# Cross-attention probabilities split before they are transposed, and transposed by a DMA instead of by TensorE

## The chip, the cores and the metric

The kernel runs on one core of one Trainium2 chip. Times are device microseconds of a whole execution. Beside the runs that are timed there is one execution with the hardware profiler; its trace has a span, from the first to the last instruction.

## What is computed

One decoder layer on x of 8 x 112 x 256 and a context of 8 x 375 x 256, in float32, with a layer norm after each of three parts: self-attention over the batch axis of the projected heads with rotary positions (16 heads of 16), cross-attention to the context (16 heads of 64), and a mixture of 8 experts, two per token, plus a shared expert. The change lies in the cross-attention:

```python
xn = _layernorm(x, ln_gamma, ln_beta)
q = (xn @ w_q).reshape(B, SQ, NUM_HEADS, DIM_HEAD)
k, v = jnp.split(context @ w_kv, 2, axis=-1)
scores = jnp.einsum('bqhd,bkhd->bhqk', q * SCALE, k)
attn = jax.nn.softmax(scores, axis=-1)
out = jnp.einsum('bhqk,bkhd->bqhd', attn, v).reshape(B, SQ, INNER)
```

## The kernel before

Three blocks run one after the other: preparation (weights split into high and low parts), attention, and the feed-forward part. The attention block treats the 8 batch entries in a loop of iterations b (0 unrolled, 1 to 6 a loop on the engines, 7 unrolled, without work for a next entry). An iteration has 8 steps s (`PAIRS`), one for each pair of cross-attention heads. Products are made of three matmuls each, from operands split in a high and a low part (`product`, lines 143 to 145).

Step s of the cross-attention runs through the engines like this:

- TensorE: `scores(b, s)` (queries x keys of two heads, 112 x 376 each, in `ps_s`), `k_project` for step s+2 into `ps_o` (L143 to L145), in some steps `v_project`, then `p_transpose(b, s-1)` (L1310: six transposes of 112 x 125 floats into `ps_t`), then `pv(b, s-2)` (L1327: 18 matmuls into another part of `ps_o`).
- VectorE: `maxima` (L993), `cpt_lo` (L997: the low half-precision part of the transposed probabilities), `k_lo`, `v_lo_cross`, `o_lo` (all through L886 and L988), and in some steps `chunk_max` (L1042).
- ScalarE: `exps` (L768, with the row sums), `k_hi`, `v_hi_cross`, `o_hi`, `cpt_hi` (L775: the high part, scaled by 2^14).
- GpSimd: `normalise` (L631: reciprocal of two sums; L635: the product of probabilities and reciprocals, in place).

The rest of an iteration belongs to entry b+1: its self-attention and its queries, cut into pieces (`FILLS`) that all engines take at places (step, place) of a table written by hand, `FILL_AT`. The pieces O0, O1 (steps 3) end in `o_norm` (L938, `o_self`). SyncE stores `o_self` to memory (L558, pieces of 64 bytes), waits until it has landed and loads it again with its rows regrouped (L564, `o_rows`). At (5, 1) TensorE transposes `o_rows` (OT, L1223) and at (5, 3) projects it (PJ). VectorE adds the residual (L953) and takes two layer norms in turn, each with a reciprocal root on GpSimd (L624) between; the second is in step 6 (`x1_moments`, `xn_norm`, L900). NT, R0, R1, Q0, Q1 follow in steps 6 and 7, and `scores(b+1, 0)` needs `qt_lo`, their end.

What sets the order: each engine runs its own list, written by hand, and waits on semaphores. VectorE's `cpt_lo(s-2)` stands before or behind `maxima(s)` by a condition `lo_first`. SyncE's queue runs `entry(b)`: load the context (L542), x (L547), two of three weight chunks, store and load o, then the third chunk. A chunk is 512 KB of expert weights; there is one buffer, `chunk`, and `load_chunk(q)` (L577) waits for `chunk_max(q-1)`. Of 27 chunks, VectorE takes three per iteration (steps 2, 3 and 7), and in iteration 7 one at the end of each step from 2 to 7:

```python
                    if not more and s >= PAIRS - LATE:
                        chunk_max(3 * b + s - PAIRS + LATE)
```

For iteration 7, SyncE has left `entry`; it loads the shared expert's weights and then has nothing but chunks to load.

## Time and profile before

| | |
|---|---|
| median of 3 runs | 754.85 us (753.52 to 756.06) |
| the profiled execution | 755.73 us |
| its span in the trace | 753.9 us |
| mean granted TensorE clock | 0.907 |
| attention block, first and last `maxima` | 112.6 and 542.5 us |
| TensorE, VectorE, ScalarE, GpSimd busy | 615.0, 480.8, 402.7, 265.2 us |

The busy times are those of instructions, not of useful work; matmuls overlap, so a mean duration of one is longer than its share of the busy time. A group's idle time is what its engine waited just before it, and behind the arrow stands the last releaser.

### The profile page before, as it was taken

To read this page: it belongs to the slowest core of one execution; us is meant where nothing else is said; L and a number is where in the kernel's file an instruction comes from. 1 tells how busy PE (TensorE), PEld (TensorE's weight loads), DVE (VectorE), ACT (ScalarE), POOL (GpSimd) and SP (SyncE) were. 2 spreads that over 40 slices of the span, in tenths; PEclk is the share of its full clock that TensorE was granted. 3 is DMA by queue.
4 is the path that set the end of the run, shared out by engine and by line. 5 is a ranking of instruction groups with operands and counts; after the bars stand their busy time and mean duration, and the time that the engine had idled before them with its cause. 6 is when DMAs were issued, how large, how long until landed. Compare 5 with 4: busy or idle time off the path is not lost. (4 is left out here: it accounts for less than half of the span.)

```text
span 753.9 us, 14298 instructions
## 1 busy us (share of the span) xinstructions
PE 615.0 (82%) x4746; PEld 483.4 (64%) x4746; DVE 480.8 (64%) x903; ACT 402.7 (53%) x989; POOL 265.2 (35%) x290
## 2 busy tenths in 40 slices
PE   4735778989999999999999999999669737899990
PEld 3524657877877877777777778777455533466660
DVE  3894336777777877776777777766649544843332
ACT  2444137567567567576577576465425414844431
POOL 3451013254254343343343353343413701133331
PEclk9965569999999999999999999999778977999995
DMA  8625110110110210210110200400324741633324
GB/s 226 210 86 175 20 47 29 42 48 28 49 37 28 60 52 28 50 44 28 48 47 28 59 36 28 124 29 29 112 98 166 248 144 47 194 62 59 58 31 109
DMA packets 58645, 57.34 MB, mean 76 GB/s; under 512 B 17266, under 2 KB 47986, under 8 KB 58610
## 3 DMA queue, kind: packets, MB, share of 16 engines
q1 hardware_dynamic: 54514, 51.68, 22.5%
q0 software_dynamic: 4096, 5.19, 4.2%
q8 instruction: 21, 0.34, 0.2%
q14 instruction: 14, 0.11, 0.1%
HBM read 46.74 MB, written 10.13 MB: 75 GB/s over the span
## 5 line engine op out<-in xcount | busy, mean ns | idle before, releaser
L631 POOL TENSOR_TENSOR c_rcp<-c_sum,neg_one 112x2 f32<-112x2 f32 x64 | 44.6, 697 | 217.2 <-ACT probs L768 217.2
L635 POOL TENSOR_TENSOR probs<-probs,c_rcp 112x750 f32<-112x750 f32 x64 | 92.0, 1437 | 5.0
L768 ACT ACTIVATE probs<-ps_s,c_neg 112x375 f32<-112x375 f32 x128 | 72.7, 581 | 22.6 <-DVE c_neg L993 22.0
L666 ACT ACTIVATE kt_hi<-ps_o 128x376 fp32r<-128x376 f32 x64 | 31.9, 498 | 76.4 <-PE ps_o L145 76.4
L1618 POOL DMA_INDIRECT moe_sum<-gsh_hi,xs_in x21 | 33.4, 1589 | 102.6 <-ACT gsh_hi L1669 69.2
L988 DVE SCALAR_TENSOR_TENSOR v_lo<-ps_vx,v_scale,v_hi 125x512 f16<-125x512 f32 x48 | 35.9, 749 | 47.0 <-ACT v_hi L760 47.0
L997 DVE SCALAR_TENSOR_TENSOR cpt_lo<-ps_t,cpt_hi 125x672 f16<-125x672 f32 x64 | 54.4, 850 | 12.5 <-ACT cpt_hi L775 12.5
L1310 PE MATMUL ps_t<-ident,probs 112*125 112x112 f32 x384 | 53.8, 277 | 8.7 <-DVE cpt_lo L997 8.6
L993 DVE TENSOR_REDUCE c_neg<-ps_s 112x2 f32<-112x750 f32 x64 | 59.5, 929 | 1.9 <-PE ps_s L145 1.7
L1938 PE MATMUL ps_h<-w_ex,xst_hi 128*128 (+1 forms) x168 | 58.5, 390 | 1.0 <-DVE xst_lo L1705 0.9
L1310 PEld LDWEIGHTS ps_t<-ident,probs 112*125 112x125 f32 x384 | 49.9, 193 | 12.6 <-POOL probs L635 7.6
L143 PE MATMUL ps_o<-ctxt_hi,w_k_lo 128*128 128x376 f32 x128 | 50.4, 394 | 8.6 <-DVE oct_lo L886 7.7
L760 ACT ACTIVATE v_hi<-ps_vx,v_scale 125x512 f16<-125x512 f32 x48 | 33.4, 696 | 37.6 <-PE ps_vx L145 37.6
L775 ACT ACTIVATE cpt_hi<-ps_t 125x672 f16<-125x672 f32 x64 | 47.3, 739 | 0.0
L145 PE MATMUL ps_o<-ctxt_hi,w_k_hi 128*128 128x376 f32 x128 | 44.6, 349 | 0.0
L144 PE MATMUL ps_o<-ctxt_lo,w_k_hi 128*128 128x376 f32 x128 | 44.5, 348 | 0.0
L1856 DVE TENSOR_TENSOR gsh_hi<-ps_g,gsh_hi 128x512 f16<-128x512 f32 x21 | 14.5, 690 | 44.4 <-ACT gsh_hi L1663 44.4
L143 PE MATMUL ps_vx<-w_v_hi,ctxt_lo 128*125 128x512 f32 x96 | 41.4, 432 | 0.3
L886 DVE TENSOR_TENSOR kt_lo<-ps_o,kt_hi 128x376 fp32r<-128x376 f32 x64 | 34.8, 543 | 9.9 <-ACT kt_hi L666 9.9
L143 PEld LDWEIGHTS ps_o<-ctxt_hi,w_k_lo 128*128 128x128 f32 x128 | 25.1, 196 | 24.8 <-issue 15.9
L144 PE MATMUL ps_vx<-w_v_lo,ctxt_hi 128*125 128x512 f32 x96 | 39.6, 412 | 0.0
L145 PE MATMUL ps_vx<-w_v_hi,ctxt_hi 128*125 128x512 f32 x96 | 39.2, 408 | 0.0
(307 smaller groups left out, 1845.3 us busy)
## 6 DMA issues: line engine op xcount, KB each, us to landing
chunk<-in_L_ffn_ew_dram SPq DMA_DIRECT2D x24, 512.0 KB, 3.5
spare<-in_L_ffn_ew_dram SPq DMA_DIRECT2D x18, 512.0 KB, 5.2
store<-in_L_ffn_ew_dram SPq DMA_DIRECT2D x6, 512.0 KB, 5.5
ctx_all<-in_ctx_dram SPq DMA_DIRECT2D x2, 1500.0 KB
ctx_raw<-in_ctx_dram SPq DMA_DIRECT2D x8, 375.0 KB
moe_in<-chunk SPq DMA_DIRECT2D x1, 2709.0 KB, 14.0
xs_in<-moe_in SPq DMA_DIRECT2D x21, 129.0 KB, 2.1
plain_raw<-in_L_xattn_w_kv_dram SPq DMA_DIRECT2D x2, 1024.0 KB, 15.9
```

The costliest lines, as they stand in the source:

```text
L143: eng.matmul(out, ll, rh, start=start, stop=False, **kw)
L144: eng.matmul(out, lh, rl, start=False, stop=False, **kw)
L145: return eng.matmul(out, lh, rh, start=False, stop=stop, **kw)
L631: pool.tensor_tensor(c_rcp[:, s % 2, :], c_sum[:, s % 2, :], neg_one[:, :], ALU.pow).then_inc(sg["c_rcp_ready"], 1)
L635: pool.tensor_tensor(p, p, r, ALU.mult).then_inc(sg["p_normed"], 1)
L768: act.activation(probs[:, s % 2, h, :], ps_s[0:N, h, 0:SK], ACT.Exp, bias=c_neg[:, s % 2, h:h + 1], accum_out=c_sum[:, s % 2, h:h + 1]).th ...
L775: act.activation(cpt[0][:, :, :, :].rearrange("p h t n -> p h (t n)"), ps_t[0:SKT, :, 0:ST * N], ACT.Copy, scale=P_SCALE).then_inc(sg["cpt ...
L988: dve.scalar_tensor_tensor(v[1][:, q, t, :], ps_v[0:SKT, :], v_scale[0:SKT, 0:1], v[0][:, q, t, :], op0=ALU.mult, op1=ALU.subtract).then_i ...
L993: dve.tensor_reduce(c_neg[:, s % 2, :], ps_s[0:N, :, 0:SK], X, ALU.max, negate=True).then_inc(sg["c_neg_ready"], 1)
L997: dve.scalar_tensor_tensor(cpt[1][:, :, :, :].rearrange("p h t n -> p h (t n)"), ps_t[0:SKT, :, 0:ST * N], P_SCALE, cpt[0][:, :, :, :].rea ...
L1310: last = pe.transpose(ps_t[0:SKT, h, t * N:(t + 1) * N], probs[:, s % 2, h, t * SKT:(t + 1) * SKT], ident[0:N, 0:N])
L1938: last = pe.matmul(out, lhs[a], rhs[b], start=start and n == 0, stop=stop and n == 2)
```

## The change

Probabilities are split into high and low half-precision parts while the queries are still the rows. GpSimd multiplies its two reciprocals by 2^14 and writes the product of probabilities and reciprocals as the high part into `p16`; VectorE makes the low part in two operations, one step earlier than `cpt_lo` stood (`p_lo(s-1)`, always right behind `maxima(s)`). Both parts of both heads, 112 x 1536 halves (each head padded to 384 keys with zeros), are transposed by one DMA of SyncE per step into `p16_t`, which `pv` reads. `p_transpose`, `cpt_hi` and `cpt_lo` go. The keys are cut at 128, 128, 119 instead of three times 125. `k_project` gets a bank of its own, so that it no longer waits for `oct_lo`, nor `pv` for `kt_lo`. SyncE's queue is written out per step.

```diff
-        cpt = half_pair(nc, ctx, "cpt", [SKT, 2, ST, N])
+        p16 = sb("p16", [N, 2, 2, 2, PW], F16)
+        p_scale = sb("p_scale", [N, 2])
+        p16_t = sb("p16_t", [P, 2, 4 * ST, N], F16)
-        ps_t = ctx.enter_context(nc.psum_tensor("ps_t", [P, 2, 512], F32))
+        ps_kt = ctx.enter_context(nc.psum_tensor("ps_kt", [P, 512], F32))
-        ps_k = ps_o[:, 0:SKP]
+        ps_k = ps_kt[:, 0:SKP]
...
+            def transpose_p(b, s):
+                n = PAIRS * b + s
+                sp.wait_ge(sg["p_lo"], n + 1)
+                if later(n - 1):
+                    sp.wait_ge(sg["pv_full"], n - 1)
+                sp.dma_start_transpose(p16_t[:, s % 2, :, :], p16[:, s % 2, :, :, :].rearrange("p a h n -> p (a h n)"))\
+                    .then_inc(sg[f"p_t{s % 2}"], 16)
...
+            store_o(0)
+            load_o(0)
+            load_ctx(1)
+            load_x(1)
+            load_chunk(0)
             for b in range(B):
-                entry(b)
-
-            sp.wait_ge(sg["qk_hi"], 4 * B)
-            sp.wait_ge(sg["qk_lo"], 3 * B)
-            sp.wait_ge(sg["k_lo"], B)
-            sp.dma_start(gw_raw[:, :, :], A["gate_w"].rearrange("(k p) e -> p k e", p=P)).then_inc(ffn_sg["gw_loaded"], 16)
-            load_weights(sp, raw, A["sw1"], A["sw2"], A["sw3"], ffn_sg["raw_loaded0"])
-            for q in range(3 * (B - 1), CHUNKS):
-                load_chunk(q)
+                more = b + 1 < B
+                for s in range(PAIRS):
+                    transpose_p(b, s)
+                    if not more and s == 0:
+                        load_ffn()
+                    if more and s == 1:
+                        load_chunk(3 * b + 1)
+                    if more and s == 2:
+                        load_chunk(3 * b + 2)
+                        store_o(b + 1)
+                    if more and s == 3:
+                        load_o(b + 1)
+                    if b + 2 < B and s == 4:
+                        load_ctx(b + 2)
+                        load_x(b + 2)
+                    if more and s == 6:
+                        load_chunk(3 * b + 3)
+                    if not more and 2 <= s < 7:
+                        load_chunk(3 * b + s - 1)
...
             def normalise(b, s):
                 pool.wait_ge(sg["c_exp"], 2 * (PAIRS * b + s) + 2)
-                pool.tensor_tensor(c_rcp[:, s % 2, :], c_sum[:, s % 2, :], neg_one[:, :], ALU.pow).then_inc(sg["c_rcp_ready"], 1)
+                if later(PAIRS * b + s - 1):
+                    pool.wait_ge(sg["p_lo"], PAIRS * b + s - 1)
+                pool.tensor_tensor(c_rcp[:, s % 2, :], c_sum[:, s % 2, :], neg_one[:, :], ALU.pow).then_inc(sg["c_rcp_part"], 1)
+                pool.wait_ge(sg["c_rcp_part"], PAIRS * b + s + 1)
+                pool.tensor_tensor(c_rcp[:, s % 2, :], c_rcp[:, s % 2, :], p_scale[:, :], ALU.mult).then_inc(sg["c_rcp_ready"], 1)
                 pool.wait_ge(sg["c_rcp_ready"], PAIRS * b + s + 1)
                 p = probs[:, s % 2]
                 r = c_rcp[:, s % 2].unsqueeze(2).to_broadcast([N, 2, SK])
-                pool.tensor_tensor(p, p, r, ALU.mult).then_inc(sg["p_normed"], 1)
+                n = PAIRS * b + s
+                if later(n - 1):
+                    pool.wait_ge(sg[f"p_t{s % 2}"], 16 * (PAIRS // 2 * b + s // 2))
+                pool.tensor_tensor(p16[:, s % 2, 0, :, 0:SK], p, r, ALU.mult).then_inc(sg["p_normed"], 1)
...
                 if later(PAIRS * b + s - 1):
-                    act.wait_ge(sg["t_full"], PAIRS * b + s - 1)
+                    act.wait_ge(sg["p_lo"], PAIRS * b + s - 1)
...
-            def cpt_lo(b, s):
-                dve.wait_ge(sg["cpt_hi"], PAIRS * b + s + 1)
...
+            def p_lo(b, s):
+                dve.wait_ge(sg["p_normed"], PAIRS * b + s + 1)
+                for h in range(2):
+                    last = dve.scalar_tensor_tensor(p16[:, s % 2, 1, h, 0:SK], probs[:, s % 2, h, :], c_rcp[:, s % 2, h:h + 1],
+                                                    p16[:, s % 2, 0, h, 0:SK], op0=ALU.mult, op1=ALU.subtract)
+                last.then_inc(sg["p_lo"], 1)
...
-                    lo_first = s in (5, 6) or (s == 1 and later(b)) or (not more and s >= 5)
-                    if lo_first:
-                        late_cpt_lo(b, s)
...
-                    if not lo_first and (s >= 2 or later(b)):
-                        late_cpt_lo(b, s)
+                    if s >= 1 or later(b):
+                        late_p_lo(b, s)
...
-            def pv(b, s, k_done):
-                pe.wait_ge(sg["cpt_lo"], PAIRS * b + s + 1)
+            def pv(b, s):
+                pe.wait_ge(sg[f"p_t{s % 2}"], 16 * (PAIRS // 2 * b + s // 2 + 1))
                 pe.wait_ge(sg["v_lo"], v_no("V02" if s < 4 else "V12", b))
-
-                pe.wait_ge(sg["kt_lo"], k_done)
```

## Rows read from the trace of the kernel before

**Rows 1.** The page, busy us (share of the span) of each engine.

```profile
PE 615.0 (82%) x4746; PEld 483.4 (64%) x4746; DVE 480.8 (64%) x903; ACT 402.7 (53%) x989; POOL 265.2 (35%) x290
```

**Rows 2.** Busy time by engine in a stretch, then clock, DMA share, GB/s.

```profile
224.00:540.00 316.00, 290.94 (x2610) 242.81 (x2609) 232.55 (x436) 203.44 (x560) 125.22 (x134) 0.99 0.16 48
```

**Rows 3.** Groups of instructions: count | busy us, mean ns | idle before.

```profile
L635 POOL TENSOR_TENSOR probs<-probs,c_rcp 112x750 f32<-112x750 f32 x64 | 92.0, 1437 | 5.0
...
L997 DVE SCALAR_TENSOR_TENSOR cpt_lo<-ps_t,cpt_hi 125x672 f16<-125x672 f32 x64 | 54.4, 850 | 12.5 <-ACT cpt_hi L775 12.5
L1310 PE MATMUL ps_t<-ident,probs 112*125 112x112 f32 x384 | 53.8, 277 | 8.7 <-DVE cpt_lo L997 8.6
...
L775 ACT ACTIVATE cpt_hi<-ps_t 125x672 f16<-125x672 f32 x64 | 47.3, 739 | 0.0
...
L631 POOL TENSOR_TENSOR c_rcp<-c_sum,neg_one 112x2 f32<-112x2 f32 x64 | 44.6, 697 | 217.2 <-ACT probs L768 217.2
...
L886 DVE TENSOR_TENSOR kt_lo<-ps_o,kt_hi 128x376 fp32r<-128x376 f32 x64 | 34.8, 543 | 9.9 <-ACT kt_hi L666 9.9
```

**Rows 4.** TensorE's waits, 160 to 590 us: total, times, longest.

```profile
PE ps_s L143 <- DVE qt_lo L886: 5.5, 7, 0.8
```

**Rows 5.** Timeline, start and duration: the way of o, and VectorE in step 4.

```profile
421.89 0.94 DVE L993 TENSOR_REDUCE c_neg<-ps_s 112x2 f32<-112x750 f32 x1
422.74 0.85 DVE L997 SCALAR_TENSOR_TENSOR cpt_lo<-ps_t,cpt_hi 125x672 f16<-125x672 f32 x1
...
422.00 0.33 SPq L558 DMA_DIRECT2D o_shuffle<-o_self  x1
424.82 0.34 SPq L564 DMA_DIRECT2D o_rows<-o_shuffle  x1
...
427.31 0.36 PE L1223 MATMUL ps_a<-ident,o_rows 112*128 112x112 f32 x2
```

**Rows 6.** Timeline: scores(b, 0), scores(b, 4), scores(b+1, 0); the first norm on GpSimd and VectorE.

```profile
390.71 0.43 PE L143 MATMUL ps_s<-kt_hi,qt_lo 64*112 64x376 f32 x2 [0.81 <-DVE qt_lo L886]
...
420.85 0.43 PE L143 MATMUL ps_s<-kt_hi,qt_lo 64*112 64x376 f32 x2
...
446.09 0.43 PE L143 MATMUL ps_s<-kt_hi,qt_lo 64*112 64x376 f32 x2 [0.82 <-DVE qt_lo L886]
...
432.03 0.56 POOL L624 TENSOR_TENSOR rstd<-mv,const_neg_half 112x1 f32<-112x1 f32 x1
...
432.81 0.41 DVE L900 TENSOR_SCALAR x<-res,mv,rstd 112x256 f32<-112x256 f32 x1
```

**Rows 7.** Timeline of the last iteration: chunk maxima of steps 2, 6, 7, and the tail.

```profile
520.51 1.21 DVE L1042 TENSOR_REDUCE w_max<-chunk 128x1 f32<-128x1024 f32 x1
...
540.64 1.22 DVE L1042 TENSOR_REDUCE w_max<-chunk 128x1 f32<-128x1024 f32 x1 [0.43 <-DMA chunk<-in_L_ffn_sw_dram]
...
545.85 1.21 DVE L1042 TENSOR_REDUCE w_max<-chunk 128x1 f32<-128x1024 f32 x1
...
553.70 0.24 PE L1327 MATMUL ps_o<-cpt_hi,v_lo 125*64 125x112 f16 x2
...
556.00 0.48 DVE L1012 SCALAR_TENSOR_TENSOR res<-ps_vx,gate_v,x_all 112x256 f32<-112x256 f32 x1 [1.05 <-PE ps_vx L145]
```

**Rows 8.** DMA issues: KB each, median us from issue to landing.

```profile
chunk<-in_L_ffn_sw_dram SPq DMA_DIRECT2D x3, 512.0 KB, 3.9
...
o_shuffle<-o_self SPq DMA_DIRECT2D x8, 112.0 KB, 2.8
o_rows<-o_shuffle SPq DMA_DIRECT2D x8, 112.0 KB, 2.0
```

**Rows 9.** Timeline: VectorE with two SBUF inputs of 256 columns, and GpSimd beside it.

```profile
393.81 0.42 DVE L886 TENSOR_TENSOR work<-store,work 112x256 fp32r<-112x256 f32 x1
395.88 1.11 DVE L886 TENSOR_TENSOR v_self<-v_all,v_self 112x256 fp32r<-112x256 f32 x1
...
395.27 1.44 POOL L635 TENSOR_TENSOR probs<-probs,c_rcp 112x750 f32<-112x750 f32 x1
```

More of the change, by code:

```diff
@@ L537, in _, with load_ctx @@
         def _(sp):
-            def entry(b):
+            def load_ctx(b):
                 if later(b):
@@ L543, in entry, with load_x @@
                     .then_inc(sg["ctx_loaded"], 16)
+            def load_x(b):
                 if later(b):
@@ L559, in entry, with load_o @@
                     .then_inc(sg["o_stored"], 16)
+            def load_o(b):
                 sp.wait_ge(sg["o_stored"], 16 * (b + 1))
@@ L565, in entry @@
                     .then_inc(sg["o_rows_loaded"], 16)
-                if b >= 1:
-                    load_chunk(3 * (b - 1) + 2)
             def load_chunk(q):
@@ new lines, in load_ffn @@
+            def load_ffn():
+                sp.wait_ge(sg["qk_hi"], 4 * B)
+                sp.wait_ge(sg["qk_lo"], 3 * B)
+                sp.wait_ge(sg["k_lo"], B)
+                sp.dma_start(gw_raw[:, :, :], A["gate_w"].rearrange("(k p) e -> p k e", p=P)).then_inc(ffn_sg["gw_loaded"], 16)
+                load_weights(sp, raw, A["sw1"], A["sw2"], A["sw3"], ffn_sg["raw_loaded0"])
+            load_ctx(0)
+            load_x(0)
+            sp.wait_ge(sg["zeroed"], 2)
+            sp.dma_start(xs.rearrange("(t p) d -> p t d", p=P), chunk[:, 0:XW].unsqueeze(1).to_broadcast([P, TILES, XW]))\
+                .then_inc(sg["slots_zeroed"], 16)
@@ L1149, in iteration @@
                         chunk_max(3 * b + s - PAIRS + LATE)
+            dve.wait_ge(sg["neg_one"], 3)
             iterations(dve, iteration)
-            cpt_lo(B - 1, 6)
+            p_lo(B - 1, 7)
             o_lo(B - 1, 6)
-            cpt_lo(B - 1, 7)
             o_lo(B - 1, 7)
@@ L1268, in k_project @@
                     pe.wait_ge(sg["kt_lo"], PAIRS * b + p)
-                if later(PAIRS * b + p - 4):
-                    pe.wait_ge(sg["oct_lo"], PAIRS * b + p - 4)
                 m = slice(p * P, (p + 1) * P)
@@ L1285, in v_project @@
                     pe.wait_ge(sg["v_lo"], v_no(f, b) - 1)
-                rows = slice(t * SKT, (t + 1) * SKT)
+                rows = slice(t * P, t * P + KEYS[t])
                 for k in range(KD):
-                    last = product(pe, ps_v[0:SKT, :], tuple(c[:, k, rows] for c in ctxt),
+                    last = product(pe, ps_v[0:KEYS[t], :], tuple(c[:, k, rows] for c in ctxt),
                                    tuple(w[:, k, 512 * q:512 * q + 512] for w in w_v), start=k == 0, stop=k == KD - 1)
@@ L1390, in place @@
                                 fill(b + 1, f)
-                    k_done = PAIRS * b + min(s + 3, PAIRS if not more else s + 3)
                     scores(b, s)
```

67 lines of the change are left out of this document (20 added, 47 removed).

## The prediction

> **What bounds the kernel now.** I read the busy table first: TensorE 82% of the span, VectorE 64%, ScalarE 53%, GpSimd 35% [rows 1]. The cross-attention loop is fuller: between 224 and 540 us TensorE works 290.94 of 316 us, at a granted clock of 0.99, so at its 2.4 GHz level [rows 2]. So removing TensorE work should pay there, if nothing else is nearly late. The groups say what goes: the six transposes of a step, 53.8 us over 64 steps, or 0.84 us a step. ScalarE's copy of them costs 47.3 us and VectorE's remainder 54.4 us [rows 3]. Then I looked for the next limit. TensorE waits at scores(b+1, 0) seven times, 5.5 us in all, for qt_lo [rows 4]. That is the end of a long chain: self-attention output, store to memory, reload with rows regrouped, transpose, projection, two layer norms, queries. One iteration lasts from 390.71 to 446.09, 55.4 us or 6.9 us a step [rows 6]. It has two sections. **A**, from scores(b, 0) to scores(b, 4) at 420.85, is 30.1 us, and TensorE leads it. **B**, from there to 446.09, is 25.2 us, and the chain leads it: o_self is stored at 422.00, the rows are loaded at 424.82, and TensorE transposes them at 427.31, only some 0.5 us after they landed [rows 5, 8].
>
> **VectorE, ScalarE, GpSimd.** cpt_lo goes (0.85 us a step) and two operations on 375 columns come. The nearest shape, kt_lo with 376 columns, takes 0.54 us, so p_lo is 1.0 us a step: +0.15 us, inside section A's VectorE idle time. ScalarE loses 0.74 us a step, off the path. GpSimd gains a multiply of two columns, priced as its neighbour of that size, 0.70 us; storing the product in half the bytes I cost at nothing (bound 0 to 0.2 us), because the row's 1.44 us is for 750 elements of two inputs either way [rows 3]. GpSimd is 35% busy, so 0.77 us with its gap matters only where someone waits: in step 5 the reciprocal root of the first norm stands behind the normalisation (432.03), and VectorE's norm starts at 432.81, just after it [rows 6]. That is +0.7 us on the chain of section B. The removed cpt_lo had hidden under the same wait.
>
> p_lo has both inputs in SBUF. In the trace v_self's low part takes 1.11 us while GpSimd's multiply runs (395.27 to 396.71), and the same 256 columns take 0.42 us beside no such neighbour [rows 9]. The Trainium skill (SBUF — State Buffer) has the rule: a VectorE instruction with two SBUF inputs and a GpSimd one that reads SBUF exclude each other for the whole instruction; the trace agrees. In step 2, p_lo(1) meets the residual addition that GpSimd starts right after normalising. I charge section A 0.6 us in all for this and for VectorE filling up. Without any such exclusion it would be about 0.3 us and the sum 2 us lower.
>
> **TensorE.** Section A drops four groups of transposes: 4 x 0.84 = 3.4 us, less 0.6, so -2.8 us. In section B dropping them buys nothing unless the chain gets shorter. Three waits go too (k_project's on oct_lo, pv's on k_done, the ones on cpt_lo), small and already inside those 2.8 us. pv's 128, 128 and 119 keys stream the same 112 columns as three times 125: nothing.
>
> **The new transfer.** It moves 112 x 1536 halves, 336 KB. No row shows a transposing DMA. Let X be the time for which one holds SyncE's queue and its rings. The store of o moves 112 KB in 64-byte pieces: issue 0.33 us, landing 2.8 us, against 2.0 us for its reload, which I take as the fixed part [rows 5, 8]. Lower bound: it goes like a plain load; the 512 KB chunk lands in 3.9 us, 1.9 over the fixed part [rows 8], so 336 KB need 1.3 us; with the best part of that hidden, 1.0. Store-like: 0.8 us for 112 KB, so 2.5 us. With pieces half as short, 4.9 us. Far upper bound: six whole stores' landings, 16.8 us. I take **X = 2.5 us**, since the store is the only row with an SBUF source in short pieces. It lands about 2.0 us later, 4.5 us after its issue. pv(s) stands at the end of step s+2, some 8 us after p_lo(s), so pv itself does not wait.
>
> **The queue order.** This is where I see the price. (1) load_o(b+1) now stands behind transpose_p(b, 3), which waits for p_lo(b, 3), behind the maximum that begins at 421.89 in VectorE's step 4. The maximum ends for its successor at 422.74 [rows 5]; plus 1.0 is 423.75; plus 0.1 for the semaphore and X is 426.35; plus 2.1 us, the rows are there at 428.45. TensorE wanted them at 427.31: +1.15 us. With 0.7 from GpSimd and 0.15 of slack before the query projection, section B grows by 1.7 us. An iteration is -2.8 + 1.7 = -1.1 us; seven of them, **-7.7 us**. (2) The other moves there are covered: load_ctx and load_x one step later are wanted a whole iteration later, and chunks 3b+1 to 3b+3 are still issued a step or more ahead of their maximum.
>
> (3) The last iteration is different. Before, the queue held only chunk loads: each was issued the moment the last maximum freed the buffer. From the end of the maximum at 520.51 to the end of the one at 545.85 there are five steps, 25.3 us, 5.1 a step, and already a wait of 0.43 us for the DMA before the one at 540.64 [rows 7]. Afterwards load_chunk(21+k) stands behind transpose_p(7, k+1), which waits for p_lo of VectorE's **own** step, at whose end the maximum of that chunk stands. So each step becomes a closed ring: maximum of scores 0.84, p_lo 1.0, semaphore 0.1, X 2.5, chunk 3.9 [rows 8], maximum 1.2 [rows 7], together 9.6 us. Five rings are 48.2 us against 25.3: **+22.9 us**. TensorE and everything behind VectorE wait. (4) Steps 0 to 2 of that iteration lose TensorE's transposes, less what VectorE hides: **-1.5 us**. The shared expert's 1.5 MB, now issued after transpose_p(7, 0), is used only after the loop; transpose_p(7, 1) may queue behind it, within the 8 us. (5) The tail: from the end of the last chunk maximum, 547.06, to res at 556.00 is 8.9 us; then p_lo 1.0, semaphore 0.1, X 2.5, landing 2.1, and pv(7) to res as before, 553.70 to 556.00, 2.3 [rows 7], make 8.0: **-0.9 us**.
>
> **Sum**: -7.7 + 22.9 - 1.5 - 0.9 = **+12.8 us**. The profiled execution took 755.73 us with a span of 753.9; it would take 768.5. The median of the runs is 754.85, so **768 us**. Per microsecond of X the sum moves by about 13 us (five rings, seven chains, the tail). It crosses zero at X = 1.5 us.
>
> **Rivals.**
> *A quick queue.* The place is the last iteration and the load of o_rows; it decides when X is under about 1.3 us. At X = 1.0 the rows come before TensorE asks and section B grows by 0.2 (-18 us over seven iterations), the rings take 8.1 us each (+15.2), steps 0 to 2 give -1.5 and the tail -2.4: -6.7 us, **748 us**. For it: the store's issue of 0.33 us, although it is cut in 112 x 16 pieces [rows 5]. Against: nothing in the trace transposes on the way, let alone at the chunk's rate. The Trainium skill (DMA: Bandwidth & Descriptors, Latency and other measured facts) gives 261 GB/s for a transposing DMA; an estimate from that page is X = 1.3 us, the edge of this rival.
> *The loop gain arrives whole.* The chain has slack that I don't see, and 56 steps give 0.84 each: -47 + 22.9 - 1.5 - 0.9 = -26.5, **728 us**. Against it: the seven waits for qt_lo.
> *Short pieces.* X = 4.9: iterations +9, rings +34.9, -1.5, tail +1.5: +44, **799 us**. For it: a transposed row arrives in pieces shorter than the store's.
> *The transfer sets the pace.* If one takes 16 us, every step lasts that long instead of 6.9: 64 x 9 = +580 us, about **1340 us**. This is also the case in which the change doesn't do what it says and moves single elements. The Trainium skill (VectorE: DVE Perf Modes, The three transpose paths) gives 1309 ns for one 128 x 128 block through the DMA against 390 ns on TensorE; twelve in a row would be 15.7 us, by that page an estimate of this rival.
>
> **Chances.** Forecast (X about 1.5 to 3.8) 43%; quick queue 25%; whole gain 8%; short pieces 16%; pace-setting transfer 8%. A measurement of this kernel tells about 0.3%, 2.3 us, from no change; 5 of the quick queue's 25 and 2 of the forecast's 43 lie within that. Faster 0.20 + 0.08 = 0.28, same 0.07, slower 0.41 + 0.16 + 0.08 = 0.65. The range leaves out the pace-setting transfer and most of the whole gain: 742 to 812 us.
>
> **What would show it.** The landing of the new DMA and the gap from its issue to the next issue on SyncE give X. In the last iteration w_max should sit 3 to 5 us behind the chunk's DMA in each of five steps, starts 9 to 10 us apart. TensorE should wait for o_rows, 1 us per iteration, and longer for qt_lo. The loop period should be near 54.3 us, its first section some 27.3. I am wrong if w_max doesn't wait, if pv waits for p16_t, or if the period falls to 50.

## The result and the profile after

The changed kernel takes **775.48 us** (median of 4 runs, 772.67 to 782.01) against 754.18 us for the kernel before on the same chip: a ratio of 1.030, 95% interval 1.023 to 1.037. The profiled execution took 772.67 us, with a span of 770.7 us; it is the fastest of the four, so what follows divides 16.8 us of growth and not the 21.3 us by which the medians differ. The time lies in the forecast range. The growth was forecast as 13 us and is 21, and not every term of the forecast holds.

The page of the kernel after (busy table, clock in 40 slices, DMA packets, and three groups of instructions):

```profile
PE 581.2 (75%) x4362; PEld 442.2 (57%) x4362; DVE 506.8 (66%) x967; ACT 362.1 (47%) x925; POOL 277.5 (36%) x356
...
PEclk9965589899999999999999999996557987999995
...
DMA packets 146709, 79.36 MB, mean 103 GB/s; under 512 B 105330, under 2 KB 136050, under 8 KB 146674
...
L1032 DVE SCALAR_TENSOR_TENSOR p<-probs,c_rcp,p 112x375 f16<-112x375 f32 x128 | 75.0, 628 | 4.3 <-POOL p L679 4.3
...
L1077 DVE TENSOR_REDUCE w_max<-chunk 128x1024 f32 (+1 forms) x27 | 32.8, 1214 | 24.1 <-DMA chunk<-in_L_ffn_sw_dram 16.2
...
L1344 PEld LDWEIGHTS ps_o<-p_t,v_lo 128*64 128x64 f16 (+1 forms) x384 | 22.9, 116 | 29.8 <-DMA p_t<-p 19.5
```

TensorE's busy time falls by 33.8 us (615.0 to 581.2), where its transposes had 53.8, and ScalarE's by 40.6 (402.7 to 362.1), where its copies had 47.3 [rows 1, 3]. VectorE's grows by 26. TensorE's clock is now at 5 to 6 tenths between 520 and 578 us, in the last iteration and just behind it.

All six chunk maxima of the last iteration, in VectorE's timeline of the kernel after (start, duration, engine, line, operation, and in brackets the idle time before it and its releaser). Before, they came 5.1 us apart, with a wait for the chunk of 0.43 us [rows 7] and one of 0.47:

```profile
516.32 1.22 DVE L1077 TENSOR_REDUCE w_max<-chunk 128x1 f32<-128x1024 f32 x1
524.67 1.22 DVE L1077 TENSOR_REDUCE w_max<-chunk 128x1 f32<-128x1024 f32 x1 [3.49 <-DMA chunk<-in_L_ffn_ew_dram]
533.42 1.22 DVE L1077 TENSOR_REDUCE w_max<-chunk 128x1 f32<-128x1024 f32 x1 [3.88 <-DMA chunk<-in_L_ffn_ew_dram]
542.25 1.22 DVE L1077 TENSOR_REDUCE w_max<-chunk 128x1 f32<-128x1024 f32 x1 [5.06 <-DMA chunk<-in_L_ffn_sw_dram]
552.08 1.22 DVE L1077 TENSOR_REDUCE w_max<-chunk 128x1 f32<-128x1024 f32 x1 [6.05 <-DMA chunk<-in_L_ffn_sw_dram]
561.00 1.22 DVE L1077 TENSOR_REDUCE w_max<-chunk 128x1 f32<-128x1024 f32 x1 [5.14 <-DMA chunk<-in_L_ffn_sw_dram]
```

SyncE's queue in the same stretch (issue and the time for which it held the queue):

```profile
527.80 1.37 SPq L584 DMA_TRANSPOSE p_t<-p  x1
529.23 0.86 SPq L575 DMA_DIRECT2D chunk<-in_L_ffn_ew_dram  x1
536.55 1.37 SPq L584 DMA_TRANSPOSE p_t<-p  x1
537.97 0.85 SPq L575 DMA_DIRECT2D chunk<-in_L_ffn_sw_dram  x1
```

One ring can be read off these two fences. The transposition is issued at 527.80 and the chunk at 529.23; the maximum starts at 533.42 and ends at 534.64; the next transposition follows at 536.55, after the maximum of the scores and p_lo. That is 1.43 + 4.19 + 1.22 + 1.91 = 8.75 us.

The span divides at the same points in both kernels:

| stretch | before | after | difference | forecast |
|---|---|---|---|---|
| start to scores(0, 0) | 111.68 | 109.73 | -2.0 | 0 |
| iterations 0 to 6, to scores(7, 0) | 391.16 | 389.95 | -1.2 | -7.7 |
| to the end of chunk maximum 21 | 18.88 | 17.86 | -1.0 | -1.5 |
| five chunk steps | 25.34 | 44.68 | +19.3 | +22.9 |
| to the last residual | 8.94 | 7.55 | -1.4 | -0.9 |
| the rest (feed-forward part) | 197.9 | 200.9 | +3.0 | 0 |
| sum | 753.9 | 770.7 | +16.8 | +12.8 |

The first line and the line before the sum are no effect of the change as far as the runs show. Ahead of scores(0, 0), the kernels below, most with the same preparation, took between 107.1 and 112.4 us. From the reduction of the chunk maxima to the end, the kernel before took 194.8 us, this one 197.9, and those below between 193.7 and 197.3; the three that keep the queue order of this one (e3, e5, e9) took 194.5, 195.9 and 194.6. Without the two lines the change costs 15.7 us in this pair of traces.

The loop has gained next to nothing: the loads of the context, over five iterations, are 279.9 us apart before and 279.8 after, 56.0 us an iteration. TensorE's waits between 160 and 508 us in the kernel after (total, times, longest) are to be held against [rows 4]:

```profile
PE ps_s L145 <- DVE qt_lo L919: 10.1, 7, 1.5
PE ps_a L1268 <- DVE ot_lo L919: 7.5, 6, 1.8
PE ps_a L1247 <- DVE pt_lo L919: 6.9, 6, 1.1
PE ps_a L145 <- DVE xnt_lo L919: 5.4, 6, 0.9
PE ps_s L145 <- ACT probs L813: 4.2, 7, 0.7
PE ps_vx L145 <- DVE res L1047: 4.1, 6, 0.7
...
PE ps_a L1255 <- DMA o_rows<-o_shuffle: 2.4, 2, 1.2
```

qt_lo was 5.5 us before. The steps, each from one start of scores to the next, in iteration 5 of the two kernels and of three of the experiments (its start in brackets):

| step | 0 | 1 | 2 | 3 | A | 4 | 5 | 6 | 7 | B |
|---|---|---|---|---|---|---|---|---|---|---|
| before (390.71) | 5.85 | 4.14 | 10.81 | 9.34 | 30.14 | 4.52 | 5.48 | 5.55 | 9.69 | 25.24 |
| after (388.06) | 5.32 | 4.12 | 10.50 | 9.10 | 29.04 | 5.40 | 7.01 | 4.74 | 10.11 | 27.26 |
| e4, fewer transposes (394.79) | 5.30 | 4.30 | 10.80 | 9.34 | 29.74 | 5.47 | 5.96 | 5.54 | 9.69 | 26.66 |
| e5, half of p_lo (386.55) | 5.33 | 4.12 | 10.50 | 9.11 | 29.06 | 5.39 | 5.74 | 5.29 | 10.15 | 26.57 |
| e14, two moves (386.45) | 5.30 | 4.11 | 10.50 | 9.09 | 29.00 | 3.90 | 5.49 | 5.97 | 10.49 | 25.85 |

One iteration is not all of them. The mean over iterations 1 to 6, and the periods of those in which TensorE's granted clock was 1.00 in every step:

| kernel | A | B | period | iterations without a fall of the clock |
|---|---|---|---|---|
| before | 30.39 | 25.72 | 56.11 | 2, 3, 5: 55.38, 55.37, 55.38 |
| after | 29.05 | 26.82 | 55.87 | none |
| e1 | 29.29 | 26.72 | 56.01 | none |
| e3 | 29.05 | 26.84 | 55.88 | 2, 3, 6: 55.71, 55.34, 55.19 |
| e4 | 30.20 | 26.77 | 56.97 | 1, 6: 55.63, 54.76 |
| e5 | 29.18 | 26.53 | 55.70 | none |
| e13 | 29.28 | 26.67 | 55.95 | none |
| e14 | 29.04 | 26.37 | 55.41 | 1: 54.63 |

(An iteration 6 is some 0.2 us shorter than another, in its step 7.) In the kernel before, the clock falls in three of the six iterations, and each is 1.5 us longer for it, 56.9 instead of 55.4. These are two starts of scores in its iteration 1: step 4 takes 6.08 us there at a mean clock of 0.72, where it takes 4.52 in iteration 5 at 1.00:

```profile
196.30 0.43 PE L143 MATMUL ps_s<-kt_hi,qt_lo 64*112 64x376 f32 x2
...
202.38 0.43 PE L143 MATMUL ps_s<-kt_hi,qt_lo 64*112 64x376 f32 x2
```

So iteration 5, from which the forecast and the table of steps take their numbers, is one of the kernel before's undisturbed ones, and in the kernel after it is one in which the clock falls. On the mean, the change makes A 1.3 us shorter and B 1.1 us longer.

### The profile page after: what moved, and what is told of

It reads as the page before. It is cut to its first block and busy times, and to the rows that moved or that the text cites. A ratio compares the mean times of both kernels' runs of the same rounds, so it can differ in the third digit from the quotient of the medians.

```text
span 770.7 us, 13622 instructions
## 1 busy us (share of the span) xinstructions
PE 581.2 (75%) x4362; PEld 442.2 (57%) x4362; DVE 506.8 (66%) x967; ACT 362.1 (47%) x925; POOL 277.5 (36%) x356
## 5 line engine op out<-in xcount | busy, mean ns | idle before, releaser
L679 POOL TENSOR_TENSOR p<-probs,c_rcp 112x750 f16<-112x750 f32 x64 | 92.1, 1440 | 7.1 <-POOL c_rcp L672 4.0
L1032 DVE SCALAR_TENSOR_TENSOR p<-probs,c_rcp,p 112x375 f16<-112x375 f32 x128 | 75.0, 628 | 4.3 <-POOL p L679 4.3
L145 PE MATMUL ps_kt<-ctxt_hi,w_k_lo 128*128 128x376 f32 x128 | 52.6, 411 | 0.0
L1344 PE MATMUL ps_o<-p_t,v_lo 128*64 128x112 f16 (+1 forms) x384 | 37.3, 232 | 16.4 <-DMA p_t<-p 16.3
L146 PE MATMUL ps_kt<-ctxt_lo,w_k_hi 128*128 128x376 f32 x128 | 45.8, 358 | 0.0
L147 PE MATMUL ps_kt<-ctxt_hi,w_k_hi 128*128 128x376 f32 x128 | 45.6, 356 | 0.0
L145 PE MATMUL ps_vx<-w_v_hi,ctxt_lo 128*128 128x512 f32 (+1 forms) x96 | 40.9, 426 | 4.7 <-DVE res L1047 4.7
L1344 PEld LDWEIGHTS ps_o<-p_t,v_lo 128*64 128x64 f16 (+1 forms) x384 | 22.9, 116 | 29.8 <-DMA p_t<-p 19.5
L1344 PE MATMUL ps_o<-p_t,v_hi 128*64 128x112 f16 (+1 forms) x768 | 39.5, 224 | 0.0
L146 PE MATMUL ps_vx<-w_v_lo,ctxt_hi 128*128 128x512 f32 (+1 forms) x96 | 39.1, 407 | 0.0
L147 PE MATMUL ps_vx<-w_v_hi,ctxt_hi 128*128 128x512 f32 (+1 forms) x96 | 39.0, 407 | 0.0
```

The lines of the kernel that those rows point to most:

```text
L145: eng.matmul(out, ll, rh, start=start, stop=False, **kw)
L146: eng.matmul(out, lh, rl, start=False, stop=False, **kw)
L147: return eng.matmul(out, lh, rh, start=False, stop=stop, **kw)
L679: pool.tensor_tensor(p16[:, s % 2, 0, :, 0:SK], p, r, ALU.mult).then_inc(sg["p_normed"], 1)
L1032: last = dve.scalar_tensor_tensor(p16[:, s % 2, 1, h, 0:SK], probs[:, s % 2, h, :], c_rcp[:, s % 2, h:h + 1], p16[:, s % 2, 0, h, 0:SK], o ...
L1344: last = pe.matmul(ps_pv[h * CHD:(h + 1) * CHD, :], v[a][0:n_k, s // 4, t, at:at + CHD], p16_t[0:n_k, s % 2, (2 * w + h) * ST + t, :], sta ...
```

## The experiments

"Before" is timed beside each group of runs (e13 and e14 ran on another chip than the rest), and the ratios are to it. The part whose cause was forecast comes first, then the loop.

### e1: the chunk loads ahead of the transpositions

```
                 for s in range(PAIRS):
+                    if not more and 2 <= s < 7:
+                        load_chunk(3 * b + s - 1)
                     transpose_p(b, s)
...
-                    if not more and 2 <= s < 7:
-                        load_chunk(3 * b + s - 1)
```

> The changed kernel, with one move in SyncE's queue: in the last iteration each chunk load stands ahead of that step's transposition instead of behind it. Theory (closed ring): the five steps between the maxima of chunks 21 and 26 fall from 44.7 us to about 28 (a chunk's landing of 4.4, its maximum of 1.2), VectorE's waits for the chunk from 23.6 us to under 5, and the time by 14 to 19 us, to about 758. Rival (the chunks only share blame: pv waits for the transposed probabilities, TensorE's waits of 15.5 us in that stage): the steps stay above 7 us each and the time falls by under 8 us.

751.13 us, ratio to before 0.995 (0.992 to 0.998): 24 us less than the kernel after, where 14 to 19 were expected, and half a per cent under before. The first and the last two of the same six maxima in its timeline:

```profile
516.99 1.21 DVE L1077 TENSOR_REDUCE w_max<-chunk 128x1 f32<-128x1024 f32 x1
...
537.30 1.22 DVE L1077 TENSOR_REDUCE w_max<-chunk 128x1 f32<-128x1024 f32 x1 [1.47 <-DMA chunk<-in_L_ffn_sw_dram]
542.66 1.22 DVE L1077 TENSOR_REDUCE w_max<-chunk 128x1 f32<-128x1024 f32 x1 [0.90 <-DMA chunk<-in_L_ffn_sw_dram]
```

Five steps of 5.1 us again, 25.7 in all instead of 44.7, with 1.5 us of wait at most. The closed ring is shown, by nothing but an order in the queue, and is worth 19.0 us in the traces. The rest of the 24 us lies outside it, 2.5 of them in the feed-forward part, which the edit does not touch. The loop stays at 279.9 us for five.

### e9: every transposition twice

```
+                sp.dma_start_transpose(p16_x[:, s % 2, :, :], p16[:, s % 2, :, :, :].rearrange("p a h n -> p (a h n)"))\
+                    .then_inc(sg[f"p_t{s % 2}"], 16)
                 sp.dma_start_transpose(p16_t[:, s % 2, :, :], p16[:, s % 2, :, :, :].rearrange("p a h n -> p (a h n)"))\
                     .then_inc(sg[f"p_t{s % 2}"], 16)
```

p16_x is a spare tile; the waits count 32 a transposition instead of 16.

> The kernel after with each transposition issued twice, the first into a spare tile. The growth of the five rings of the last iteration (44.7 us after), divided by five, is X, the time for which one transposition holds the queue and the rings. By its issue alone X is 1.36 us: rings 51.5, about +7 us. If the transfer also holds the rings that the chunk needs, X is 2 to 3.5 us (rings 55 to 62), and the loop grows too: the kernel at 785 to 810.

797.21 us (1.053, 1.043 to 1.064). The first and the last maximum of the rings, in its timeline:

```profile
532.49 1.21 DVE L1080 TENSOR_REDUCE w_max<-chunk 128x1 f32<-128x1024 f32 x1
...
585.11 1.22 DVE L1080 TENSOR_REDUCE w_max<-chunk 128x1 f32<-128x1024 f32 x1 [6.97 <-DMA chunk<-in_L_ffn_sw_dram]
```

Five rings take 52.6 us instead of 44.7, so **X = 1.6 us**. The instruction alone holds the queue for 1.36, so little more is added in the rings: they come near the first expectation (51.5). The loop follows the second: it pays too, 57.8 us an iteration, and so the whole lies in 785 to 810. The prediction had X at 2.5.

### e2: the rows first

On e1:

```
+                    if more and s == 3:
+                        load_o(b + 1)
                     transpose_p(b, s)
...
-                    if more and s == 3:
-                        load_o(b + 1)
```

> As e1, and the reload of o_rows ahead of the transposition of step 3 as well. Theory: the reload was late in two of six iterations only (2.4 us in all), so this gives 0 to 3 us on top of e1, and the loop period stays between 55.3 and 56.0 us. Rival (the prediction's step: section B is led by this reload, 1.15 us each): 6 to 8 us on top of e1, period 54.8.

754.49 us (0.999, 0.996 to 1.002): no gain on e1 (0.995, 0.992 to 0.998), and so not the 6 to 8 us of the prediction's step. The queue's view of it shows why the load itself came no earlier, 4.70 us after scores(4) at 416.65 as against 4.69 in the kernel after:

```profile
416.26 0.37 SPq L575 DMA_DIRECT2D chunk<-in_L_ffn_ew_dram  x1
417.80 0.33 SPq L556 DMA_DIRECT2D o_shuffle<-o_self  x1
421.35 0.34 SPq L564 DMA_DIRECT2D o_rows<-o_shuffle  x1
```

The store has taken 3.55 us instead of the 2.82 of before (422.00 to 424.82 [rows 5]), behind a chunk that the new order issues 1.5 us ahead of it. In the kernel after, the load stands right behind the transposition of step 3, which is issued 3.25 us after scores(4) and holds the queue until 4.5. Either of the two, the late store or the transposition, puts the load at 4.7 us, so taking one away gains nothing.

### e3 and e8: unused transposes against the clock

```
+            def warm(n):
+                for _ in range(n):
+                    pe.transpose(ps_w[:, 0:P], ident[:, :], ident[:, :])
...
             def fill(b, f):
+                if later(b):
+                    warm({"O1": 6, "C1": 10}.get(f, 0))
...
+                    if s == 0 and later(b):
+                        warm(8)
                     scores(b, s)
```

e3 is this on the kernel after:

> The changed kernel with TensorE work added that nobody uses: transposes of the identity into a spare bank, 6 ahead of O1, 10 ahead of C1, 8 ahead of scores(b+1, 0), where TensorE waits for VectorE. Theory (lost clock): in the changed kernel the granted clock falls to 0.52 to 0.73 after these waits, which makes the work behind them twice as long; with the waits filled it stays at 1.00, the loop period falls from 56.0 by 1.5 to 3 us, the time by 9 to 20 us, although 24 transposes (some 3 us) are added per iteration. Rival (the dips cost nothing, since VectorE leads): period the same within 0.5 us, or longer by up to 3 us, time the same or slower.

768.54 us (1.020, 1.014 to 1.026). Its granted clock over the loop is 1.00, 1.00, 0.97 and 0.97, where the kernel after has 0.94 to 0.97, but five iterations take 280.0 us, as before. The gain on the kernel after, 7 us by the medians and 6.2 in the profiled executions, does not come from the loop: in the traces 2.7 us of it lie ahead of scores(0, 0) and 3.4 in the feed-forward part, both of which the edit leaves as they are. Its waits between 160 and 508 us:

```profile
PE ps_a L1282 <- DVE xn L934: 6.7, 6, 1.3
PE ps_a L1256 <- DMA o_rows<-o_shuffle: 5.9, 4, 2.1
...
PE ps_s L145 <- DVE qt_lo L920: 2.9, 7, 0.4
```

e8 is the same on e1:

> The chunk loads of the last iteration ahead of the transpositions, together with unused transposes on TensorE ahead of three of its waits in the loop. Alone, the first gave 751.13 and the second -7 us. If the two gains are separate: 744. If the second one came from outside the loop or is hidden once the rings are gone: 750 to 752, with a loop period of 55.8 in both cases.

751.74 us (0.995, 0.991 to 0.998), the same as e1, as the second expectation had it. A clock held up turns into waits for xn and for the rows: here the lower clock is paid in time that TensorE otherwise waits. That does not hold for the kernel before, where each fall of the clock costs its 1.5 us in full.

### e4: before, with one transposition of six

On the kernel before, five of a step's six transposes on TensorE are left out, so that the probabilities used are partly stale and the output is not the layer's.

```
                 for h in range(2):
                     for t in range(ST):
+                        if (h or t) and not (isinstance(b, int) and b == 0 and s == 0):
+                            continue
```

> The kernel before with one of the six transposes of each step left (the first step keeps all six); the others' results are stale, so the output is not the layer's. It prices TensorE's transposes alone: ScalarE, VectorE and SyncE do what they did. Theory (the chain through o_rows leads half of an iteration, and the clock may dip): 0.7 us a step removed gives at most 2.5 us an iteration, 5 to 18 us in all. Rival (TensorE leads everywhere): 64 x 0.7 = 35 to 45 us faster.

755.92 us (0.998, 0.994 to 1.001), five iterations 287.1 us instead of 279.9. Both expectations, 5 to 18 us and 35 to 45 us, missed. Its waits between 160 and 508 us:

```profile
PE ps_s L143 <- DVE qt_lo L886: 9.4, 7, 1.4
...
PE ps_a L1215 <- DVE pt_lo L886: 6.2, 6, 1.0
PE ps_a L1236 <- DVE ot_lo L886: 5.2, 6, 0.9
```

The same waits in the kernel before, where qt_lo has 5.5 us [rows 4]:

```profile
PE ps_a L1215 <- DVE pt_lo L886: 2.9, 6, 0.5
PE ps_a L1236 <- DVE ot_lo L886: 2.3, 6, 0.4
```

This run says most on the loop: 0.7 us of TensorE work less in each step, nothing else touched, and no gain. VectorE and GpSimd have no more to do here than before, and yet the waits for qt_lo, pt_lo and ot_lo grow by 10.1 us. The transposes had stood between a matmul and the next use of its result, and had covered the round trip through ScalarE's high part and VectorE's low part.

The granted clock is lower as well (0.91 to 0.97 over the loop), and the iterations keep the two apart. Two of the six ran at 1.00 throughout and took 55.6 and 54.8 us, against 55.4 in the kernel before: of 5.6 us of work left out, 0.2 arrive on the mean, with no fall of the clock at all. That is the cover alone. In the other four the clock falls to 0.54 to 0.69 in step 4, and they take 56.4 to 59.4 us: that is where the 7 us of the five iterations went.

### e5: half of p_lo

The low part is computed for head 0 only; head 1's stays zero.

```
-                for h in range(2):
+                for h in range(1):
                     last = dve.scalar_tensor_tensor(p16[:, s % 2, 1, h, 0:SK], probs[:, s % 2, h, :], c_rcp[:, s % 2, h:h + 1],
```

> The kernel after with the low part computed for one of the two heads (the other head's low part is left at zero), so VectorE is 0.56 us a step shorter, 4.5 us an iteration; nothing else moves. Theory V (VectorE, in its fixed order, now sets the loop's pace): the loop period falls by 3 to 4.5 us from 55.96, TensorE's waits for qt_lo, ot_lo, pt_lo and xnt_lo shrink, and with five rings 0.6 us shorter the whole is 22 to 35 us under the kernel after, about 743 to 753. Rival C (TensorE at its lower granted clock, or another chain such as the stores and loads, sets it): the period stays within 0.5 us of 55.96 and only the five rings give their 3 us, about 772.

769.58 us (1.019, 1.010 to 1.029). Of the 4.5 us an iteration that VectorE no longer works, 0.5 arrive (277.5 us for five between the loads of the context), or 0.2 on the mean of the six iterations. Section A of iteration 5 is the same to 0.02 us; the rings shrink from 8.94 to 8.37 us, just the 0.56 of one head. VectorE's busy time does not set the loop.

### e10: the low part on GpSimd

On e1: GpSimd scales in place, ScalarE copies the high part, GpSimd subtracts.

```
-                pool.tensor_tensor(p16[:, s % 2, 0, :, 0:SK], p, r, ALU.mult)
+                pool.tensor_tensor(p, p, r, ALU.mult)
+                act.activation(p16[:, s % 2, 0, :, 0:SK], probs[:, s % 2], ACT.Copy)
+                pool.tensor_tensor(p16[:, s % 2, 1, :, 0:SK], probs[:, s % 2], p16[:, s % 2, 0, :, 0:SK], ALU.subtract)
```

> The chunk loads first, and the split of the probabilities taken from VectorE altogether: GpSimd scales them in place, ScalarE copies the high part (750 columns, about 0.75 us a step, where it had gained 0.74), GpSimd subtracts (1.44 us a step more). VectorE loses 1.12 us a step, 9 us an iteration. Theory V: the period falls by 4 to 9 us, 710 to 730 us in all, and TensorE becomes fuller than before (its waits under 3 us an iteration). Theory V with the port: GpSimd's longer busy time holds VectorE's instructions with two SBUF inputs, so that 2 to 4 us of it come back: 730 to 745. Rival C: the period stays near 55.9, about 751.

799.42 us (1.058, 1.049 to 1.067), 62.0 us an iteration. All expectations missed: 9 us of VectorE work less makes it 6 us slower. From its page:

```profile
L668 POOL TENSOR_TENSOR p<-probs,p 112x750 f16<-112x750 f32 x64 | 100.4, 1569 | 159.3 <-ACT p L826 159.3
...
L826 ACT ACTIVATE p<-probs 112x750 f16<-112x750 f32 x64 | 52.8, 825 | 10.8 <-POOL probs L683 10.7
```

GpSimd and ScalarE now wait for each other once a step, in orders that also hold the exponentials and the norms. Which of the two sets the 62 us was not tried.

### e11: fills inside O1

On e1, a 128-column transpose behind each of the first seven pairs of O1's short matmuls:

```
                     last = pe.matmul(out[:, 0:VS], pt[1][:, j, :], v_self[:, bb, r, 0:VS], start=False, stop=True)
+                    if i == 1 and j < 7 and later(b):
+                        pe.transpose(ps_w[:, 0:P], ident[:, :], ident[:, :])
```

> Chunk loads first, and seven unused 128-column transposes between the pairs of short matmuls (34 and 18 columns) of O1, the last work of step 3. In the kernel after, TensorE's granted clock is 0.56 to 0.59 from 417.1 to 420.6 us, behind these, and step 4 takes 5.40 instead of the 4.52 of before, though its transposes are gone; transposes ahead of O1 did not change that. Theory K (the short matmuls behind a longer wait take the clock down): the clock stays at 1.00, step 4 takes about 3.7 us, O1 0.5 us more; unless the rows of o are then waited for, the period falls from 55.9 to about 54.8 and the whole from 751 to about 743. Rival: step 4 stays near 5.4 or its gain turns up as a wait for o_rows and ot_lo in step 5, and the period stays at 55.9.

762.53 us (1.009, 1.006 to 1.011): worse. The clock (third column from the end) in two windows behind O1, which began at 421:

```profile
424.00:427.00 3.00, 3.00 (x12) 2.54 (x13) 2.71 (x7) 0.00 (x0) 0.00 (x0) 0.50 0.75 174
427.00:430.00 3.00, 3.00 (x24) 2.07 (x24) 0.68 (x2) 1.91 (x6) 0.89 (x2) 0.61 0.60 114
```

TensorE was busy, and yet in this iteration it went to its 1.2 GHz level earlier and for longer, and steps 3 and 4 took 1.2 and 0.9 us more than in the kernel after. Two more of the six iterations look like it, and one has no fall in step 4. Filling the gaps inside O1 did not hold the clock up; what takes it down stays open.

### e12: T3 ahead of V11

On e1, in step 3; the same on ScalarE and VectorE for v_hi_cross and v_lo_cross:

```
-                    if s != 2 and s in V_AT and (s < 6 or more):
+                    if s not in (2, 3) and s in V_AT and (s < 6 or more):
                         v_project(b if s < 6 else b + 1, V_AT[s])
                     place(2)
...
-                    if s == 2:
+                    if s in (2, 3):
                         v_project(b, V_AT[s])
```

> Chunk loads first, and in step 3 the transposes T3 ahead of the value projection V11 instead of behind it, on all three engines that follow this order; no work is added or removed. Theory F (the six transposes of a step had covered round trips through ScalarE and VectorE; without them TensorE waits for the same results): V11's 2.8 us now cover the round trip to O1, TensorE's wait for pt_lo (1.15 us in step 3) goes, step 3 falls from 9.10 to about 8.0 and the period from 55.9 to about 54.9, the whole from 751 to 743 to 745. Rival: another engine's order sets step 3 (V11's high and low parts now come later on ScalarE and VectorE), the wait moves to ps_s or qt_lo, and the time stays at 751 or rises.

759.71 us (1.005, 1.002 to 1.008), and not the 743 to 745 of the theory. The wait for pt_lo goes, but step 3 falls only to 8.83, since T3 now waits 0.73 us for the bank that o_sum reads. And one wait grows, in TensorE's timeline:

```profile
375.67 0.63 PE L1261 MATMUL ps_a<-ident,o_rows 112*128 112x112 f32 x2 [2.35 <-DMA o_rows<-o_shuffle]
```

The matmuls go by earlier and the rows do not: this iteration takes 56.9 us, and the six 56.6 on the mean. To cover one round trip uncovers the next.

### e13 and e14: the chain of section B

e13 is e2 with the chunk 3b+2 behind load_o, where the kernel before had it; e14 has, besides, p_lo(4) behind ot_lo on VectorE:

```
                     if more and s == 2:
-                        load_chunk(3 * b + 2)
                         store_o(b + 1)
+                    if more and s == 3:
+                        load_chunk(3 * b + 2)
```

```
-                    if s >= 1 or later(b):
+                    if s != 5 and (s >= 1 or later(b)):
                         late_p_lo(b, s)
...
                     if s != 2:
                         place(1)
+                    if s == 5:
+                        late_p_lo(b, s)
```

> Chunk loads first in the last iteration, the load of o_rows ahead of transposition 3, and the load of chunk 3b+2 behind both, as in the kernel before, in place of ahead of the store of o. In the run with the rows first, the load of o_rows was still issued 3.55 us after the store, against 2.82 before; the chunk's transfer, issued 1.5 us ahead of the store, is what differs. If it is that: the load is issued some 4.0 us after scores(4) again instead of 4.7, the period falls by about 0.7 us and the whole from 751-754 to 746 to 749. If the transpositions' own pieces hold the rings: the store still takes 3.5 us and the time stays.

> The same, and in step 5 the low part p_lo(4) behind ot_lo and ctxt_lo on VectorE. In the kernel after, ot_lo starts 1.95 us after the transposes of o_rows, against 1.18 before, because p_lo(4) ahead of it waits for GpSimd's product of its own step. If section B's chain is what sets the period: 0.8 us an iteration less than the run beside it, together 1.5 us, period 54.4, the whole 740 to 744. If the loop is set elsewhere (section A, the clock): no difference between the two, and the freed time turns up as a wait for xn or xnt_lo.

e13: 750.49 us (0.994, 0.991 to 0.997). The store is back at 2.83 us and the load is issued 3.98 us after scores(4), as expected:

```profile
418.16 0.33 SPq L556 DMA_DIRECT2D o_shuffle<-o_self  x1
420.99 0.34 SPq L564 DMA_DIRECT2D o_rows<-o_shuffle  x1
```

But TensorE still waits 1.80 us for ot_lo, five iterations take 280.0, and the whole is not the 746 to 749 expected. So the chunk ahead of the store was what kept the load of the rows late in e2, and the late rows were not what the time hung on. e14: **748.22 us** (0.989, 0.986 to 0.992), five iterations 276.8 us. ot_lo starts at 422.37, 0.86 us ahead of p_lo:

```profile
422.37 0.38 DVE L920 TENSOR_TENSOR ot_lo<-ps_a,ot_hi 128x224 fp32r<-128x224 f32 x1
...
423.23 1.12 DVE L1033 SCALAR_TENSOR_TENSOR p<-probs,c_rcp,p 112x375 f16<-112x375 f32 x2
```

Section B is 25.9 us in the iteration shown, 0.6 over before; neither has a fall of the clock in B's step 4. On the mean of six it is 26.4, against 26.7 in e13. The gain is less than expected (740 to 744), because 1.6 us of wait for xn come in its place. The step from e13 to e14 is 2.3 us by the medians, with single runs from 747.6 to 755.0 and from 743.0 to 754.2, and one fall of the clock in e13's iteration 1 has 1.5 of the 3.3 us between their loops: that moving p_lo(4) helps is likely, its size is not settled. e14 is still the fastest of the kernels, 1.1% under before.

## Why the prediction was right, and where its steps were not

**The last iteration (3): right, with one size too large and two too small.** The wait stands where it was put and the order alone makes it (e1). The ring was forecast at 9.6 us and measured 8.94: X is 1.6, not 2.5, p_lo 1.12, not 1.0, and from the chunk's issue to its maximum it is 4.2 us, where I had 3.9. (The terms as I wrote them add up to 9.54 us, so that five rings are 47.7 and not 48.2.) X was drawn from the store of o, the nearest row with short pieces, and that was the wrong neighbour: the transposing instruction is long in its issue (1.36 us) and short in its landing (3.5 us in the middle of 64; 4.5 forecast). The Trainium skill (DMA: Bandwidth & Descriptors, Latency and other measured facts) has 261 GB/s for a transposing DMA whose middle dimension is not contiguous, by estimate 1.3 us for this one. The time that the queue is held, 1.36 us, is near it; that this is the transfer's own time no run shows. The estimate of 15.7 us, from one block's 1309 ns in the Trainium skill (VectorE: DVE Perf Modes, The three transpose paths) taken twelve times in a row, is not what happens: all twelve have landed after 3.5 us.

**That the total came out near is in part luck.** By the forecast's own formula X = 1.6 gives about 1 us over before, hardly a change; the trace is 16.8 us over. The rings were put 3.6 us too dear, and the loop's gain of 7.7 us came to 1.2; the two errors point opposite ways. What failed is the step "an iteration is -2.8 + 1.7 = -1.1 us; seven of them, -7.7": the mean iteration is 0.2 us shorter. The step took the period of before from one iteration, 55.4 us; three of its six are 56.9, and their mean is 56.1.

**Section A: -2.8 forecast, -1.1 measured in iteration 5 (-1.3 on the mean).** I took TensorE to lead it, so that 0.84 us a step would arrive, less what VectorE hides. VectorE hides nothing of it (e5: 29.06 against 29.04). Of the 3.4 us, 2.0 went into waits: 0.65 for the exponentials ahead of scores(2), 0.69 for the residual in step 2, and 1.15 instead of 0.49 for pt_lo in step 3; the steps themselves got shorter by some 3.1. The same waits for pt_lo, qt_lo and ot_lo come when the transposes are left out of the kernel before, also where its clock does not fall (e4). A TensorE 92% busy was read as the bound; it was filled with work that covered round trips.

**Section B: +1.7 forecast, +2.0 measured in iteration 5 (+1.1 on the mean), and made of other terms.** The load of the rows of o is issued 4.69 us after scores(4) instead of 3.97, so 0.72 us later and not 1.15. The transposition ahead of it, as forecast, puts it there, but so does by itself the chunk ahead of the store (e2), and only e13, without either, has 3.98. The chunk was my queue order (2), "the other moves there are covered", which missed that a store of 2.8 us takes 3.5 behind a chunk. And TensorE waits for the rows in two iterations of six, 1.2 us each, those in which step 4 took 3.9 us at a clock of 1.00. In iteration 5 it comes to the transposes of the rows 0.77 us later on its own, without a wait in the trace, since its step 4 takes 5.4 us at a clock of 0.68. The forecast had no term for that. GpSimd's +0.7 did not come: its added multiply takes 0.20 us and the normalisation ends at 429.31, ahead of the variance at 430.00. In its place ot_lo stands behind p_lo(4), which waits for GpSimd's product of its own step. The chain of the two kernels, from scores(4) at 420.85 and 417.10. Before, behind the transposes of the rows at 427.31 [rows 5]:

```profile
428.49 0.38 DVE L886 TENSOR_TENSOR ot_lo<-ps_a,ot_hi 128x224 fp32r<-128x224 f32 x1
```

After:

```profile
424.33 0.35 PE L1255 MATMUL ps_a<-ident,o_rows 112*128 112x112 f32 x2
...
425.30 0.60 DVE L1032 SCALAR_TENSOR_TENSOR p<-probs,c_rcp,p 112x375 f16<-112x375 f32 x1
...
426.28 0.38 DVE L919 TENSOR_TENSOR ot_lo<-ps_a,ot_hi 128x224 fp32r<-128x224 f32 x1
```

From the transposes of the rows to ot_lo it was 1.18 us and is 1.95: 0.77 more. This is the term that e14 is made to take back. Another 0.36 us lie in xnt_lo, the same 224 columns in 0.94 us before and in 1.30 after. Two groups of the loop, 206 to 430 us, of the kernel after show the port:

```profile
L919 DVE TENSOR_TENSOR v_self<-v_all,v_self 112x256 fp32r<-112x256 f32 x4 | 6.2, 1562 | 0.4
...
L919 DVE TENSOR_TENSOR xnt_lo<-xnt_f,xnt_hi 128x224 fp32r<-128x224 f32 x4 | 5.2, 1300 | 1.9 <-ACT xnt_hi L775 1.9
```

In e10, where GpSimd's work falls at other times, the same two take 0.43 and 0.69 us. In the iteration shown, v_self and xnt_lo end 0.25 to 0.28 us after GpSimd's product does, in the kernel before and in the one after. The Trainium skill (SBUF — State Buffer, Who interferes with whom) has VectorE instructions with two SBUF inputs and GpSimd instructions that read SBUF exclude each other; the trace agrees, and the price was where I had not looked for it.

**Right:** pv does not wait for p16_t in the loop; the tail (-0.9 forecast, -1.4 measured); p_lo at 628 ns an operation against the row's 543; GpSimd's product at 1.44 us with half the bytes to write. **A sign of being wrong that came:** in the last iteration pv does wait for p16_t, 13.4 us in four waits between 500 and 560 us, which the forecast had excluded. In e1 it still waits 12.1 us there and the rings' 19 us are gone, so these waits are not what the 19 us come from. The rivals *short pieces* and *pace-setting transfer* fell with X (a packet of the transposing DMA has 250 bytes on the mean, not fewer than the store's 64), *the loop gain arrives whole* fell in section A, and the *quick queue* came nearest in X (1.6 against 1.0 to 1.3) without its time, because its loop gain is missing.

**Open:** five iterations take 279.8 to 280.0 us in the kernels before, after, e1, e3, e8 and e13 alike. The means of A and B leave 0.2 us an iteration between before and after, and single iterations differ by up to 1.5 us within one execution, so agreement to 0.2 us in 280 is in part chance. What brings the clock down in one iteration and not in the next is not known. Not tried: the kernel before with the order of e14, and the kernel after with only the chunk 3b+2 moved.

## What to carry to other kernels

Ask of work that you take off a busy engine what it stood in front of: where each result makes a round trip over two other engines, the instruction between is cover, and its time is not on offer (try it first by leaving the work out, as e4). Of a load put behind something in a queue, follow what that something waits for to its end; if it waits for the engine that consumes the load, the loop is closed and every transfer's latency is paid in full. A transfer also delays the ones issued behind it, so in a queue count what goes ahead of a short, urgent store. And take the period of a loop from all its iterations: here three of six were 1.5 us longer than the one that was read.

## What the hardware showed unexpectedly

- **A transposing DMA**, in the view of p_t in the kernel after (ns of issue as least, median, most; then first and last start):

```profile
L584 SPq DMA_TRANSPOSE p_t<-p x64: 1260/1359/3216, 119.4 to 563.3; - x64
...
DMA to landing us min/median/max: 3.4/3.5/7.3
```

  1.36 us of queue for 112 x 1536 halves (a load of 512 KB: 0.37 us alone, 0.86 behind one of these), 88,064 more packets (1376 each), and still the data are there after 3.5 us (7.3 at most).
- **A lower clock costs little in one kernel and its full price in another.** TensorE's granted clock drops in the kernel after from 2.4 GHz towards the 1.2 GHz level behind O1 (0.56 in this window, the third column from the end; 0.59 in the next):

```profile
417.00:419.00 2.00, 2.00 (x10) 1.53 (x10) 1.61 (x5) 0.00 (x0) 0.00 (x0) 0.56 0.35 116
```

  Step 4 takes 5.4 us with such a dip and 3.9 without it (iterations 1 and 6 of the same kernel), but the iterations of e3 and e8, with fewer dips, are as long on the mean. In the kernel before, a dip makes its iteration 1.5 us longer, and in e14 one in step 4 makes section B 26.7 to 27.3 us where it is 25.6 to 25.9. With less work for TensorE there were more dips: three iterations of six have one before, all six after, and e4, with four, has the longest; with more work in one place, in e11, the one behind O1 is deeper (0.55 to 0.58 over step 4 in three iterations, against 0.68 to 0.70).
- **GpSimd's reciprocal is a dear operation for its size:** two columns take 0.70 us as a power and 0.20 as a multiply.
